# Local transformers: the feed-forward's normalisation moved onto tokens, with new orders of work

## The chip, the cores and the metric

One core of a Trainium2 chip runs the whole kernel. The metric is the device time of one execution in microseconds (us); the median of three is given. The profile is one further execution, taken by the hardware profiler.

## What is computed

Eight layers act on x of 8 sequences x 256 tokens x 128 channels; before each, x is normalised over its channels, and the layer's result is added to x. Layers 2 and 4 are the same local transformer of six blocks (`DEPTH`). One block is, for each sequence (`LN_EPS` is 1e-5):

```
x = attn_layer(shift_tokens(x), Wqkv, q_scale, k_scale, Wo) + x
t = shift_tokens(x)                      # the upper 64 channels come from the token before
mu  = t.mean(-1);  var = ((t - mu)**2).mean(-1)
xn  = (t - mu) / sqrt(var + 1e-5) * g + bln
a, gate = split(xn @ W1 + b1)
x = (a * gelu(gate)) @ W2 + b2 + x
```

The attention has 16 heads of 64 in windows of 32 tokens, l2-normalised and rotated queries and keys, and a softmax. The other layers are a state-space scan, a dense and a linear attention, a per-head attention and two quantised feed-forward layers. The change touches the local transformers, and the normalisation that stands ahead of every one of the eight layers.

## The kernel before

**Layout.** In the local transformer activations lie with channels on the partitions and tokens along the free dimension (`net.zT`, 128 x 256 for a sequence). There are 48 sequence-blocks (`SEQS` = 6 blocks x 8 sequences) in each of the two layers, and each passes through the stages below. `pipeline` (L1031) runs 54 iterations on every engine. In iteration n a step with lag k works on sequence-block n - k, so `run(score, 4, 0)` is the score product of block n - 4. Five engines each have an `iteration` with an order written out by hand; they are coupled by semaphores alone, and an engine works strictly in its order. Lag 2 to 4 is shift, projection, rotation and turning of q and k; lag 4 and 5 scores, softmax and the weighted sum; lag 6 the output projection and the feed-forward.

**TensorE (L1356 and on).** Twelve projections of 512 columns (`project`, `project_v`), four `turn_qk` and four `turn_probs` (16 transposes of 64 rows each), four `score`, four `weigh`, two halves of `out_project`, three `up`, one `down`. The 512-column products run as two matmuls on two halves of the output partitions (`COLUMNS`). The lists `PROJECTIONS` and `PAIRS_OF_BANKS` state in which order the PSUM banks are handed on, and so what each product waits for.

**The feed-forward's normalisation.** `out_project` leaves the attention's output in the PSUM bank `fb`. On VectorE `residual1` (L1571) makes three additions: the shifted residual `xs2` in two halves of 64 channels, and the unshifted residual `z1`. On TensorE `centre` (L1307) multiplies `xs2` by the centring matrix. On ScalarE `square2` (L1440) writes the square and a copy `cen`. `variance` (L1314) sums the squares with four narrow products, `add_eps` (VectorE), `std` and `spread_std` (POOL: a power, and a diagonal matrix 128 x 256) follow, and `spread` (L1322) multiplies ones by that diagonal, which puts each token's factor on all partitions. `affine` (VectorE, L1585) multiplies it by gain and `cen`; `bias_xn` (ScalarE) adds the bias and writes `xn`, the input of `up`.

**The layers' normalisation.** `normalise` (L243) treats 2048 tokens as four quarters. Last in it TensorE spreads the factors for quarters 0 and 1, then 2 and 3, and VectorE multiplies quarter after quarter (L348 to L351).

**SyncE.** `next_wo`, `next_w1`, `next_w2`, `next_wqkv` (L1072 to L1098) reload weights once per block of eight sequences, each behind the last use of the old ones, and `move_v` moves parts of v.

## Time and profile before

| | us |
|---|---|
| median of 3 executions | 4160.24 (4156.2 to 4161.15) |
| the profiled execution, its own time | 4153.05 |
| its span in the profile | 4151.3 |
| TensorE busy | 3819.6 (92%) |
| VectorE / ScalarE / POOL busy | 3628.6 / 3311.8 / 3092.3 |

The two local transformers take the stretches from about 492 to 2057 us and from about 2204 to 3770 us. PE is TensorE's matmul, PEld its weight load, DVE VectorE, ACT ScalarE, POOL GpSimd and SP SyncE. A view of the timeline gives the start, the duration, the engine, the line, the output and inputs, the count, and in brackets the idle time ahead of it with what ended it. Durations of successive instructions on one engine overlap, so the cost of one is read as the distance to the next one's start. An fp32 matmul shows as two records, a transpose as one.

### The profile page before, as it was taken

What the parts mean: (1) busy time and instruction counts of PE and PEld (TensorE: products, weight loads), DVE (VectorE), ACT (ScalarE), POOL (GpSimd) and SP (SyncE); (2) the same over time, 40 slices, a digit from 0 to 9 for tenths busy, and PEclk for the clock granted to TensorE, in tenths of its full rate; (3) what the DMA queues carried; (4) which work ended last, traced back from release to release, by engine and by line L of the source; (5) the groups of instructions that cost most, each with busy time, mean ns of one, the idle gap of its engine ahead of it and who ended that gap; (6) DMA issues with size and microseconds to landing.
All of it is one profiled execution on the core that took longest, in us unless ns stands there. A gap on an engine that the chain in (4) does not pass through costs nothing. (4 is left out here: it accounts for less than half of the span.)

```text
span 4151.3 us, 141232 instructions
## 1 busy us (share of the span) xinstructions
PE 3819.6 (92%) x52643; PEld 2278.6 (55%) x52643; DVE 3628.6 (87%) x11433; ACT 3311.8 (80%) x10465; POOL 3092.3 (74%) x3901
## 2 busy tenths in 40 slices
PE   5888889999999999999867999999999999996686
PEld 2333356666666666666553666666666666663464
DVE  7999899999999999999477999999999999984646
ACT  6888589999999999999515999999999999983122
POOL 3999788888888888888396888888888888862324
PEclk8999999999999999999998999999999999997888
DMA  1000111111111111111002111111111111110000
GB/s 29 1 1 1 48 25 26 50 33 28 53 28 43 41 36 38 30 41 26 20 0 58 31 28 43 38 43 33 38 43 28 50 33 31 30 33 3 6 3 11
DMA packets 78607, 122.74 MB, mean 30 GB/s; under 512 B 26024, under 2 KB 47204, under 8 KB 77924
## 3 DMA queue, kind: packets, MB, share of 16 engines
q1 hardware_dynamic: 77924, 113.71, 10.2%
q8 instruction: 419, 6.86, 0.7%
q14 instruction: 264, 2.16, 0.2%
HBM read 35.56 MB, written 1.05 MB: 9 GB/s over the span
## 5 line engine op out<-in xcount | busy, mean ns | idle before, releaser
L1123 POOL TENSOR_TENSOR local_qk<-local_qk,local_rb 128x512 f32<-128x512 f32 x768 | 977.4, 1278 | 228.5 <-DVE local_rb L1532 228.0
L1420 ACT ACTIVATE local_pr<-local_tb,local_nmax 128x96 f32<-128x96 f32 x3072 | 1002.2, 355 | 126.7 <-DVE local_nmax L1551 116.1
L1551 DVE CUSTOM_DVE_ANT_0 local_tb<-local_tb,local_mask,local_rinv 128x96 f32<-128x96 f32 x3072 | 785.4, 319 | 78.6 <-PE local_tb L1253 75.5
L1228 PE MATMUL local_pj<-local_wqkv,local_xs 128*64 128x512 f32 x3072 | 797.6, 609 | 29.0 <-DVE local_xs L1516 15.0
L1157 POOL TENSOR_TENSOR local_pr<-local_pr,local_rsum 128x384 f32<-128x384 f32 x768 | 622.8, 827 | 194.9 <-DVE local_rsum L1558 194.9
L1420 ACT ACTIVATION_READ_ACCUMULATOR local_pr<-local_tb,local_nmax 128x1 f32 x3072 | 676.5, 221 | 0.0
L1529 DVE TENSOR_TENSOR local_qk<-local_pj,local_rope 128x512 f32<-128x512 f32 x768 | 524.0, 682 | 97.7 <-ACT local_sq L1403 94.4
L1403 ACT ACTIVATE local_sq<-local_pj 128x512 f32<-128x512 f32 x768 | 472.6, 615 | 111.5 <-PE local_pj L1228 111.5
L1532 DVE TENSOR_TENSOR local_rb<-local_pj,local_rope 128x512 f32<-128x512 f32 x768 | 523.3, 681 | 0.7 <-POOL local_qk L1123 0.7
L1539 DVE TENSOR_REDUCE local_ss<-local_sq 128x8 f32<-128x512 f32 x768 | 519.3, 677 | 0.0
L1277 PEld LDWEIGHTS local_ob<-local_prT,local_v 128*64 128x64 f32 x12288 | 414.9, 138 | 175.5 <-issue 163.0
L1277 PE MATMUL local_ob<-local_prT,local_v 128*64 128x64 f32 x12288 | 428.2, 223 | 4.2 <-DVE local_oT L1568 4.2
L1551 DVE DVE_READ_ACCUMULATOR2_ANT local_nmax<- 128x1 f32 x3072 | 430.1, 140 | 2.0
L1428 ACT ACTIVATE local_prT<-local_tb 128x512 f32<-128x512 f32 x768 | 412.9, 634 | 0.7 <-PE local_tb L1264 0.5
L1239 PE MATMUL local_pj<-local_wqkv,local_xs 128*64 128x512 f32 x1536 | 400.8, 600 | 1.6 <-DVE local_rb L1532 1.6
L1129 POOL TENSOR_TENSOR local_qk<-local_qk,local_rinv 128x512 f32<-128x512 f32 x384 | 396.3, 1042 | 0.0
L1253 PEld LDWEIGHTS local_tb<-local_kT,local_qT 64*64 64x64 f32 x12288 | 266.2, 133 | 194.7 <-ACT local_prT L1428 76.3
L1302 PE MATMUL local_fb<-local_oT,local_wo 128*64 128x256 f32 x3072 | 368.0, 382 | 1.4 <-DVE net_zT L1601 1.4
L777 POOL TENSOR_TENSOR mamba_scan_drive<-mamba_u,mamba_scan_b_all 128x512 f32<-128x512 f32 x256 | 320.1, 1276 | 52.4 <-ACT mamba_scan_b_all L747 48.9
L1344 PE MATMUL local_fb<-local_xn,local_w 128*64 128x256 f32 x2304 | 313.1, 393 | 11.0 <-DVE local_g L1595 4.7
L1292 PEld LDWEIGHTS local_tb<-net_ident,local_qk 64*128 64x128 f32 x6144 | 221.3, 139 | 185.7 <-issue 147.9
L1253 PE MATMUL local_tb<-local_kT,local_qT 64*64 64x96 f32 x12288 | 320.6, 248 | 0.3 <-ACT local_kT L1437 0.3
(450 smaller groups left out, 7283.0 us busy)
## 6 DMA issues: line engine op xcount, KB each, us to landing
local_v<-local_v SPq DMA_DIRECT2D x288, 256.0 KB, 3.9
local_wqkv<-L_ffn_Wqkv_dram SPq DMA_DIRECT2D x72, 256.0 KB, 3.1
local_wo<-L_ffn_Wo_dram SPq DMA_DIRECT2D x12, 512.0 KB, 4.1
local_w<-L_ffn_W_dram SPq DMA_DIRECT2D x12, 341.0 KB, 3.0
mamba_parts<-mamba_in_low SPq DMA_DIRECT2D x24, 64.0 KB, 2.0
local_w<-L_ffn_W_dram SPq DMA_DIRECT2D x12, 128.0 KB
y_dram<-store_xtok SPq DMA_DIRECT2D x4, 256.0 KB, 2.8
local_oT<-rope_dram SPq DMA_DIRECT2D x2, 256.0 KB, 2.7
```

The source lines that it names most:

```text
L1123: nc.gpsimd.tensor_tensor(qk[:, u, :], qk[:, u, :], rb[:, u % 2, :], ALU.add).then_inc(s["summed"], 1)
L1157: nc.gpsimd.tensor_tensor(at, at, view(rsum[:, k // 2, k % 2, 0:1], [[1, 4], [0, KW]]), ALU.mult).then_inc(s["weighted"], 1)
L1228: ins = nc.tensor.matmul(bank[own, :], xs[:, par, u // 4 * P + own.start:u // 4 * P + own.stop], wqkv[:, dep % 2, u % 4 * BANK:(u % 4 + 1) ...
L1253: ins = nc.tensor.matmul(sc[h][low * QB:(low + 1) * QB, i * KW:(i + 1) * KW], qT[own, par, p, q:q + QB], kT[own, par, p, q:q + KW], start= ...
L1277: ins = nc.tensor.matmul(ob[h * DH:(h + 1) * DH, i * P + low * QB:i * P + (low + 1) * QB], v[:, par, V_BLOCK[2 * t + low], 2 * (4 * half + ...
L1403: nc.scalar.activation(sq[:, u % 2, :], projection_bank("rotated", u)[:, :], ACT.Square).then_inc(s["squared"], 1)
L1420: ins = nc.scalar.activation(pr[:, (NU * c + k) % PR_RING, i, WIN:WIN + KW], scores[:, i * KW:(i + 1) * KW], ACT.Exp, scale=-1.0, bias=nma ...
L1428: nc.scalar.activation(prT[:, kk % PT_RING, low, :], pair_of_banks("probs", kk)[low][:, :], ACT.Copy).then_inc(s["probs_copied"], 1)
L1529: nc.vector.tensor_tensor(heads8(qk[:, u, :]), heads8(bank[:, :]), cosines, ALU.mult)
L1532: nc.vector.tensor_tensor(rb[:, u % 2, :].rearrange("p (h a c) -> p h a c", a=2, c=DH // 2), swapped, sines, ALU.mult).then_inc(s["rotated ...
L1539: nc.vector.tensor_reduce(ss[:, par, 8 * u:8 * u + 8], heads8(sq[:, u % 2, :]), AX.X, ALU.add).then_inc(s["summed_sq"], 1)
L1551: ins = nc.vector.tensor_tensor_reduce(at, at, mask[:, k // 4, :], rinv[:, par, head:head + 1], 3.0e38, ALU.add, ALU.min, nmax[:, k, i:i + 1])
```

## The change

In the feed-forward the normalisation is done with tokens on the partitions. `residual1` makes one addition, into a `z1` with a column of zeros in front. `turn_z` transposes `z1` on TensorE in two halves of 64 channels; the upper half reads one column earlier, which is the shift. VectorE takes mean and variance of each of the two token tiles with `bn_stats` and `bn_aggr`. POOL adds epsilon, takes the power and makes scale and bias for each token (`affine`). ScalarE applies them (`scale_tokens`), `turn_x` transposes back, and `bias_xn` applies gain and bias for each channel. Since the bias comes out as plus mean times factor and the scale as minus the factor, POOL turns the sign of the gains once. `centre`, `variance`, `spread`, `square2`, `add_eps`, `spread_std` and the old `affine` are gone. All five hand-written orders and the two bank lists are new. In `normalise` the pairs are (0,3) and (1,2), and quarter 3 is multiplied on POOL from a copy that ScalarE makes.

```diff
+SPREAD_PAIRS = ((0, 3), (1, 2))
@@ normalise
+            pool.wait_ge(moved, 1)
+            pool.wait_ge(kept, NC)
+            nc.gpsimd.tensor_tensor(part(z, NC - 1), part(z, NC - 1), part(sq, NC - 1), ALU.mult)
...
-            for pair in ((0, 1), (2, 3)):
+            for pair in SPREAD_PAIRS:
...
+            act.wait_ge(spread, 1)
+            nc.scalar.activation(part(sq, NC - 1), p_bc[:, NC - 1, :], ACT.Copy).then_inc(moved, 1)
...
-            for q in range(NC):
+            for q in range(NC - 1):
                 dve.wait_ge(kept, q + 1)
-                dve.wait_ge(spread, q // 2 + 1)
+                dve.wait_ge(spread, 1 if q == 0 else 2)
@@ lists
+PAIRS_OF_BANKS = [("qk", 4, 1), ("probs", 5, 1), ("score", 4, 0), ("probs", 5, 2), ("qk", 4, 2), ("qk", 4, 3),
+         ("probs", 5, 3), ("qk", 3, 0), ("probs", 4, 0), ("score", 4, 1), ("score", 4, 2), ("score", 4, 3)]
+PROJECTIONS = [("rotated", 3, 2), ("v_ready", 4, 2), ("v_ready", 4, 3), ("rotated", 3, 3), ("rotated", 3, 4), ("rotated", 3, 5),
+         ("rotated", 3, 6), ("rotated", 3, 7), ("rotated", 2, 0), ("v_ready", 3, 0), ("v_ready", 3, 1), ("rotated", 2, 1)]
@@ SyncE iteration
                 run(move_v, 0, 0)
+                run(next_w1, 2, 0)
+                run(next_w2, 2, 0)
                 run(next_wo, 1, 0)
-                run(next_w1, 1, 0)
                 run(next_wqkv, -1, 0)
-                run(next_w2, 1, 0)
@@ POOL
             def std(e, par, _):
+                pool.wait_ge(s["var_in"], 2 * e + 2)
+                need(pool, s["tokens_ready"], e)
+                nc.gpsimd.tensor_scalar(deviation[:, :], mean_var[:, :, 1], LN_EPS, None, ALU.add).then_inc(s["eps_added"], 1)
+                pool.wait_ge(s["eps_added"], e + 1)
+                nc.gpsimd.tensor_tensor(rstd[:, :], deviation[:, :], net.minus_half[:, 0:2], ALU.pow).then_inc(s["root_ready"], 1)
+                pool.wait_ge(s["root_ready"], e + 1)
+                nc.gpsimd.tensor_tensor(affine[:, :, :], view(mean_var[:, 0, 0:1], [[3, 2], [2, 2]]), view(rstd[:, 0:1], [[1, 2], [0, 2]]),
+                                        ALU.mult).then_inc(s["std_ready"], 1)
@@ TensorE
+            def turn_z(e, par, h):
+                rows = COLUMNS[h]
+                if h:
+                    pe.wait_ge(s["z1_turned"], 2 * e + 1)
+                else:
+                    pe.wait_ge(s["z1_ready"], e + 1)
                 for t in range(2):
+                    ins = nc.tensor.transpose(fb[:, t * P + rows.start:t * P + rows.stop], z1[rows, par, 1 - h + t * P:1 - h + (t + 1) * P], net.ident[rows, rows])
+                ins.then_inc(s["z1_turned"], 1)
+
+            def turn_x(e, par, h):
...
+                    ins = nc.tensor.transpose(fb[:, L + t * P + rows.start:L + t * P + rows.stop], xt[rows, t, :], net.ident[rows, rows])
@@ TensorE iteration, whole, in its new order
+ out_project 6,1 | project 3,2 | turn_z 6,0 | turn_qk 4,1 | turn_z 6,1 | turn_probs 5,1 | project_v 4,2
+ score 4,0 | weigh 5,0 | project_v 4,3 | project 3,3 | weigh 5,1 | project 3,4 | turn_probs 5,2
+ turn_x 6,0 | turn_qk 4,2 | turn_x 6,1 | project 3,5 | weigh 5,2 | up 6,0 | project 3,6 | turn_qk 4,3
+ turn_probs 5,3 | up 6,1 | project 3,7 | turn_qk 3,0 | turn_probs 4,0 | project 2,0 | up 6,2
+ score 4,1 | score 4,2 | project_v 3,0 | down 6,0 | weigh 5,3 | project_v 3,1 | score 4,3
+ project 2,1 | out_project 5,0
@@ ScalarE
+            def scale_tokens(e, par, _):
+                act.wait_ge(s["std_ready"], e + 1)
+                need(act, s["x_turned"], 2 * e)
+                for t in range(2):
+                    ins = nc.scalar.activation(xt[:, t, :], fb[:, t * P:(t + 1) * P], ACT.Identity, scale=affine[:, t, 1:2], bias=affine[:, t, 0:1])
+                ins.then_inc(s["tokens_ready"], 1)
@@ VectorE
+                need(dve, s["z1_turned"], 2 * (e - 1))
                 need(dve, s["z_ready"], B + e - 1)
+                nc.vector.tensor_tensor(z1[:, e % 2, 1:1 + L], z[:, e % B, :], fb[:, 0:L], ALU.add).then_inc(s["z1_ready"], 1)
+
+            def stats(e, par, _):
+                dve.wait_ge(s["z1_turned"], 2 * e + 2)
+                for t in range(2):
+                    nc.vector.bn_stats(moments[:, t, :], fb[:, t * P:(t + 1) * P]).then_inc(s["moments_ready"], 1)
+
+            def aggregate(e, par, _):
+                for t in range(2):
+                    dve.wait_ge(s["moments_ready"], 2 * e + t + 1)
+                    need(dve, s["std_ready"], e)
+                    nc.vector.bn_aggr(mean_var[:, t, 0:2], moments[:, t, :]).then_inc(s["var_in"], 1)
@@ VectorE iteration, whole, in its new order (ss is sum_squares)
+ maxima 5,7 | recip 5,2 | rotate 3,1 | residual1 6,0 | ss 3,1 | recip 5,3 | ss 3,2 | stats | aggregate
+ rotate 3,2 | maxima 4,0 | copy_o 5,0 | maxima 4,1 | shift_in 2,0 | rotate 3,3 | ss 3,3 | copy_o 5,1
+ recip 4,0 | rotate 3,4 | ss 3,4 | copy_o 5,2 | rotate 3,5 | ss 3,5 | rotate 3,6 | ss 3,6 | gate 6,0
+ ss 3,7 | rotate 3,7 | gate 6,1 | gate 6,2 | maxima 4,2 | maxima 4,3 | rotate 2,0 | maxima 4,4
+ maxima 4,5 | residual2 6,0 | copy_o 5,3 | maxima 4,6 | ss 2,0 | recip 4,1
```

ScalarE's new order begins with the copies of the last turns and the squares, then `exps` 5,2 to 5,7, and has `scale_tokens` ahead of `exps` 4,0 and `bias_xn` ahead of `square` 3,5. The table of exp and that of gelu are still each loaded once in an iteration.

## Rows read from the trace of the kernel before

**Rows 1.** The page, part 1: busy time, share of the span, instructions.
```profile
PE 3819.6 (92%) x52643; PEld 2278.6 (55%) x52643; DVE 3628.6 (87%) x11433; ACT 3311.8 (80%) x10465; POOL 3092.3 (74%) x3901
```
**Rows 2.** Windows: busy time of each engine in one period of 31.42 us.
```profile
core 0: us, PE busy (x) PEld busy (x) DVE busy (x) ACT busy (x) POOL busy (x), PEclk, DMA share, GB/s
985.00:1016.42 31.42, 31.42 (x520) 19.39 (x518) 29.46 (x107) 29.40 (x102) 25.53 (x36) 1.00 0.13 36
```
**Rows 3.** Line L1450 (`bias_xn`) in two stretches of the second transformer: first and last start.
```profile
L1450 ACT ACTIVATE local_xn<-local_fb,local_cols x4: 474/474/476, 2299.3 to 2393.6; 128x256 f32<-128x256 f32 x4
...
L1450 ACT ACTIVATE local_xn<-local_fb,local_cols x2: 473/473/473, 3735.0 to 3755.8; 128x256 f32<-128x256 f32 x2
```
**Rows 4.** Timeline of PE: the three products that go, and their neighbours.
```profile
1020.07 0.60 PE L1311 MATMUL local_fb<-local_xs,net_center 128*64 128x256 f32 x4
1020.60 0.89 PE L1253 MATMUL local_tb<-local_kT,local_qT 64*64 64x96 f32 x32
...
1022.40 0.35 PE L1318 MATMUL local_fb<-net_mean,local_sq 128*64 128x1 f32 x8
1022.61 1.92 PE L1228 MATMUL local_pj<-local_wqkv,local_xs 128*64 128x512 f32 x8
...
1025.28 0.60 PE L1326 MATMUL local_fb<-local_diag,net_ones 128*64 128x256 f32 x4
1025.82 0.71 PE L1292 MATMUL local_tb<-net_ident,local_qk 64*128 64x64 f32 x16
1026.37 0.67 PE L1264 MATMUL local_tb<-net_ident,local_pr 64*128 64x64 f32 x16
```
**Rows 5.** The page, part 5: the costliest weight loads of a turn.
```profile
L1292 PEld LDWEIGHTS local_tb<-net_ident,local_qk 64*128 64x128 f32 x6144 | 221.3, 139 | 185.7 <-issue 147.9
```
**Rows 6.** Timeline of DVE: what goes (additions, affine) in one period.
```profile
1018.25 0.86 DVE L1576 TENSOR_TENSOR local_xs<-net_zT,local_fb 64x256 f32<-64x256 f32 x2
1019.14 0.42 DVE L1578 TENSOR_TENSOR local_z<-net_zT,local_fb 128x256 f32<-128x256 f32 x1
...
1025.94 0.49 DVE L1589 SCALAR_TENSOR_TENSOR local_fb<-local_fb,local_cols,local_cen 128x256 f32<-128x256 f32 x1
```
**Rows 7.** Timeline of ACT: `square2`, and what follows its copy (left out).
```profile
1020.71 0.40 ACT L1442 ACTIVATE local_sq<-local_fb 128x256 f32<-128x256 f32 x1
...
1021.26 0.62 ACT L1411 ACTIVATE local_v<-local_pj 128x512 f32<-128x512 f32 x1
```
**Rows 8.** Timeline of POOL: the diagonal matrix.
```profile
1023.83 0.61 POOL L1151 TENSOR_TENSOR local_diag<-net_ident,local_deviation 128x256 f32<-128x256 f32 x1
```
**Rows 9.** Timeline of PE, around the end of the feed-forward.
```profile
1003.86 1.55 PE L1253 MATMUL local_tb<-local_kT,local_qT 64*64 64x96 f32 x64
1005.34 1.08 PE L1344 MATMUL local_fb<-local_xn,local_w 128*64 128x256 f32 x8
1006.25 1.03 PE L1239 MATMUL local_pj<-local_wqkv,local_xs 128*64 128x512 f32 x4
...
1012.05 0.71 PE L1292 MATMUL local_tb<-net_ident,local_qk 64*128 64x64 f32 x16
```
**Rows 10.** Timeline of DVE in the same stretch: gates, one unit of maxima, `residual2`.
```profile
1006.74 0.86 DVE L1595 SCALAR_TENSOR_TENSOR local_g<-local_fb,local_cols,local_g 128x256 f32<-128x256 f32 x2
1007.53 0.31 DVE L1551 CUSTOM_DVE_ANT_0 local_tb<-local_tb,local_mask,local_rinv 128x96 f32<-128x96 f32 x1
...
1008.47 0.85 DVE L1516 TENSOR_REDUCE local_xs<-net_zT 64x256 f32<-64x256 f32 x2
...
1010.42 0.48 DVE L1601 SCALAR_TENSOR_TENSOR net_zT<-local_fb,local_cols,local_z 128x256 f32<-128x256 f32 x1
```
**Rows 11.** The end of `normalise` ahead of the second transformer: timelines of ACT and DVE.
```profile
2200.48 1.08 ACT L328 ACTIVATE net_zT<-local_ln_p_cen 128x512 f32<-128x512 f32 x2
...
2201.92 2.48 DVE L351 TENSOR_TENSOR net_zT<-net_zT,local_ln_p_bc 128x512 f32<-128x512 f32 x4 [2.03 <-PE local_ln_p_bc L319]
```
**Rows 12.** The page, part 5: a POOL product of 128x512.
```profile
L1123 POOL TENSOR_TENSOR local_qk<-local_qk,local_rb 128x512 f32<-128x512 f32 x768 | 977.4, 1278 | 228.5 <-DVE local_rb L1532 228.0
```

More of the change, by code:

```diff
@@ L264, in normalise @@
         p_weights = p_bc[:, 1, :]
[L265 to L266 removed]
+        cleared, centred, squared, summed, kept, roots, turned, copied, spread, moved = (
+            net.sem(f"{tag}_ln_{n}") for n in ("cleared", "centred", "squared", "summed", "kept", "roots", "turned", "copied", "spread", "moved"))
         x = net.xT[:, :, :].rearrange("p b l -> p (b l)")
@@ L1175, in iteration @@
                 run(scale, 4, 2)
-                run(scale, 4, 3)
                 run(norm_p, 5, 2)
                 run(norm_p, 5, 3)
+                run(scale, 4, 3)
                 run(add_parts, 3, 0)
@@ L1181, in iteration @@
                 run(norm_p, 5, 4)
+                run(std, 6, 0)
+                run(norm_p, 5, 5)
                 run(add_parts, 3, 1)
+                run(add_parts, 3, 2)
+                run(norm_p, 5, 6)
                 run(scale, 4, 7)
-                run(norm_p, 5, 5)
-                run(add_parts, 3, 2)
-                run(std, 6, 0)
-                run(spread_std, 6, 0)
                 run(add_parts, 3, 3)
-                run(norm_p, 5, 6)
-                run(add_parts, 3, 4)
                 run(norm_p, 5, 7)
@@ L1193, in iteration @@
                 run(norm_p, 4, 1)
+                run(add_parts, 3, 4)
                 run(add_parts, 3, 5)
@@ L1477, in iteration @@
                 run(copy_probs, 5, 2)
+                run(copy_v, 4, 2)
                 run(copy_probs, 5, 3)
-                run(square2, 6, 0)
-                run(copy_v, 4, 1)
+                run(scale_tokens, 6, 0)
                 run(exps, 4, 0)
+                run(copy_v, 4, 3)
                 run(square, 3, 3)
@@ L1484, in iteration @@
                 run(square, 3, 4)
-                run(bias_xn, 6, 0)
-                run(copy_qk, 4, 4)
-                run(copy_qk, 4, 5)
                 run(copy_probs, 5, 4)
                 run(copy_probs, 5, 5)
+                run(copy_qk, 4, 4)
+                run(bias_xn, 6, 0)
                 run(square, 3, 5)
+                run(copy_qk, 4, 5)
                 run(gelu, 6, 0)
+                run(gelu, 6, 1)
                 run(square, 3, 6)
@@ L1607, in iteration @@
             def iteration(run):
-                run(add_eps, 6, 0)
+                run(maxima, 5, 7)
+                run(recip, 5, 2)
+                run(rotate, 3, 1)
+                run(residual1, 6, 0)
+                run(sum_squares, 3, 1)
+                run(recip, 5, 3)
+                run(sum_squares, 3, 2)
+                run(stats, 6, 0)
+                run(aggregate, 6, 0)
+                run(rotate, 3, 2)
+                run(maxima, 4, 0)
                 run(copy_o, 5, 0)
-                run(recip, 5, 3)
                 run(maxima, 4, 1)
+                run(shift_in, 2, 0)
                 run(rotate, 3, 3)
-                run(affine, 6, 0)
                 run(sum_squares, 3, 3)
+                run(copy_o, 5, 1)
+                run(recip, 4, 0)
                 run(rotate, 3, 4)
-                run(recip, 4, 0)
-                run(copy_o, 5, 1)
                 run(sum_squares, 3, 4)
+                run(copy_o, 5, 2)
                 run(rotate, 3, 5)
```

175 lines of the change are left out of this document (63 added, 112 removed).

## The prediction

> **What bounds the kernel now.** I read the page's first part, then windows over one period of the local transformer, then the timeline of each engine in that period. The page makes TensorE the busiest engine, with VectorE near it [rows 1]. A share over the span mixes stages, so the next view is one period of the pipeline: in 31.42 us TensorE has no idle time at all, at a granted clock of 1.00; VectorE is busy 29.46 us, ScalarE 29.40, POOL 25.53 [rows 2]. Busy TensorE might still hide waits, since the ends of matmuls are modelled, so I looked at distances between starts: a 16-transpose group costs 0.55 us wherever another such group follows, and the whole sequence repeats without a gap. So one period is TensorE's own work, and what is taken from TensorE comes off the time, as long as VectorE (1.96 us of slack) and ScalarE (2.02 us) can follow.
>
> How many periods count: the first `bias_xn` of the second transformer starts at 2299.3 and the 47th at 3735.0 [rows 3]. That is 1435.7 us for 46 distances, which is 45 at 31.42 and one short one of 22 in the drain. With two transformers 90 periods are bound by TensorE. Filling and draining are not, for there the engines wait for each other in turn.
>
> **What TensorE loses.** `centre` holds it from 1020.07 to 1020.60, 0.53 us; `variance` from 1022.40 to 1022.61, 0.21; `spread` from 1025.28 to 1025.82, 0.54 [rows 4]. Together 1.28 us in a period.
>
> **What TensorE gains.** Four groups of two transposes (`turn_z` twice, `turn_x` twice), eight in all, each with 64 rows and 128 columns of weights and 64 moving columns: the very form of `turn_qk`. There 16 take 0.55 us [rows 4], 0.034 us each. But `turn_qk` alternates between the lower and the upper 64 rows, so that two run side by side; each half has 8 in 0.55 us, 0.069 us each. The new groups keep to one half. The lower bound is 0.034 each, 0.28 us in all, if they slip beside the turns of the other half, next to which the new order puts them. The upper bound takes the whole duration of such a weight load, 0.139 us [rows 5], for each of the eight: 1.11 us. I take 0.069, the rate that one half is seen to keep: 0.55 us. TensorE's period becomes 31.42 - 1.28 + 0.55 = 30.69, a gain of 0.73 us.
>
> Against this stands a rule. The trace shows eight weight loads of 0.139 us for one half inside 0.55 us [rows 4, 5], so they overlap with something of their own half or end early. The Trainium skill (TensorE: Matmul & The Clock Gate, Part 3, The mechanism) says that a weight load overlaps running matmuls only where its row group differs, and its section on LDWEIGHTS makes 128 columns about 107 ns. By that the eight would cost at least 0.86 us and the gain would be 0.42 us a period. The trace of `turn_qk` does not bear it out, since one half would then need 0.86 us where 0.55 is measured; the result it points to is weighed as the first rival.
>
> **VectorE.** Gone are the two half additions, 1018.25 to 1019.14, 0.89 us, and the affine, about 0.40 of its 0.49 [rows 6], and the narrow `add_eps`, left out of the sum; the third addition of 0.42 stays. New are two `bn_stats` over 128 elements and two `bn_aggr` over 6. The trace has neither. Nearest are a 256-element addition at 0.42 [rows 6] as an upper end, and a unit of four maxima over 96 elements each, 0.94 us or 0.24 apiece [rows 10], as the lower end for the first. I take 0.25 for a `bn_stats` and 0.18 for a `bn_aggr`: 0.86 in all, 1.7 at worst. VectorE loses 1.3 and gains 0.86: from 29.46 to about 29.0, at worst 29.9. Still under 30.69.
>
> **ScalarE.** `square2` with its copy holds it from 1020.71 to 1021.26, 0.55 us [rows 7]. `scale_tokens` is two activations of 128 elements with two per-partition operands; a 256-element one costs 0.27 to 0.40 [rows 7], so two cost 0.4 to 0.8, taken as 0.55. Even. `bias_xn` gets a scale operand, at most 0.1. The two table loads stay two. So ScalarE remains at about 29.4 of 30.69: its slack shrinks from 2.0 to 1.3 us. This is the thinnest place of the forecast.
>
> **POOL.** The 0.61 us diagonal [rows 8] goes, two operations on 2 and 4 elements with a wait between come, about 0.5. With 25.5 us of 31.42 it has room. Nothing gained or lost; queued behind `std` are `norm_p` 5,5 and additions, due several us later. The sign of the gains is turned once, while filling.
>
> **The new waits on TensorE.** An engine in a fixed order stands still if one operand is late, so I walked three places of the new order. First, `out_project` 5,0 now closes the iteration and needs `residual2`. From the end of `up` 6,2 TensorE has two scores, 1.48, and then the same six groups as between 1006.25 and 1012.05, 5.80: 7.28 us [rows 9]. VectorE meanwhile does two gates, 0.79, four units of maxima at 0.94, one rotation of two 512-element operations at 0.62 [rows 11], and `residual2`, 0.48 [rows 10]: 6.27, and 0.1 for the signal. Margin 0.9 us; before, VectorE had only two units of maxima and `shift_in` there. Second, `turn_z` 6,0 stands one projection behind (0.9, as the `up` from 1005.34 to 1006.25 [rows 9], both four fp32 records' worth of 512 columns) `out_project`: signal, addition 0.42, signal, about 0.6. Margin 0.3, if VectorE is free by then. Third, the chain from `turn_z` through statistics, POOL and `scale_tokens` has nine groups of TensorE, 0.55 to 0.93 us each, some 7 us, before `turn_x`, and needs about 3.5 plus POOL's queue. None of them stops TensorE by my count, but none is wide. Each costs its overrun 90 times.
>
> **SyncE.** The reloads of w1 and w2 are issued ahead of that of wo and one step later in SyncE's order, and `move_v` of the next block stands behind them. All of them are waited for in the order in which TensorE uses the weights up, once in eight periods, and have most of a period before the next use; the DMA engines are busy for 0.13 of the time [rows 2]. Cost nothing; if the cover fails, a few us ten times in the run.
>
> **`normalise`, eight times.** VectorE multiplies four quarters from 2201.92 for 2.48 us, to 2204.40 [rows 11]. With three it ends at about 2203.8. ScalarE is free at 2201.56 [rows 11], copies the fourth in 0.6 from 2201.92, and POOL's product of 128x512, 1.28 us [rows 12], ends at about 2203.9. So 0.5 us eight times, 4 us; from nothing (POOL slow to start) to 5.
>
> **The sum.** 90 x 0.73 = 66, plus 4, is 70 us. Filling and draining are taken as even, with 5 us to either side: the chain of the last block loses two products and gains two turns with waits. The profiled execution has 4153.05 us around a span of 4151.3; it would become about 4083. The median before, 4160.24, lies 7 above it, and the same saving gives 4090.
>
> **Rivals.** A measurement of this kernel can tell about 0.2%, 8 us, from no change.
>
> *Turns are dear.* Each of the eight waits for its own weight load, 0.139 us [rows 5]. TensorE's period is 31.42 - 1.28 + 1.11 = 31.25: 90 x 0.17 = 15, with 4 of `normalise` 19 us, 4141. For it speaks that two in a row share a half, against it the 0.55 us of `turn_qk`. Chance 0.12. The skill's rule above, at 107 ns, would land between this and the forecast.
>
> *ScalarE becomes the bound.* It idles 2.02 us a period now [rows 2], while TensorE never does. If the waits of the new order leave it as much, its period is 29.4 + 2.0 = 31.4, nothing is gained in the pipeline, and only the 4 us of `normalise` remain: 4156. TensorE would then show idle time of 0.7 us a period. For it: the slack is short and exps and maxima wait for each other. Against: most of that idle time is waiting for TensorE's products, which come sooner. Chance 0.08; the change would in effect not do what it says.
>
> *`out_project` waits for `residual2`.* The margin of 0.9 us above is used up by VectorE running late behind gates and maxima, which wait for `gelu` and so for ScalarE. It has to be late by 0.9 + 0.73 = 1.6 us to cost more than is gained; at 2.0 the period is 31.8, so 90 x 0.4 = 36 slower, less 4: 4192. Chance 0.08.
>
> **How the numbers follow.** The forecast, 4090, has a chance of 0.72. Its own range runs from 4060 (turns at 0.034: 90 x 1.0 = 90, `normalise` 5, ends 5) to about 4120 (half of the gain lost to small waits). The range of 8 in 10 reaches on to the dear turns: 4060 to 4141. Faster by over 0.2%: forecast, dear turns and a little of the second rival, 0.86. Within 0.2%: the rest of the second, 0.06. Slower: 0.08.
>
> **What will show it.** Windows of one period after: a period near 30.7 with TensorE still without idle time. The timeline of TensorE: each pair of turns 0.14 us to the next start; 0.28 would be the dear case. VectorE near 29.0, ScalarE near 29.4 busy. The waits: no long one of `out_project` for `residual2`, nor of `turn_z` for `z1`. The last quarter of `normalise` ending 0.5 us earlier. I am wrong if TensorE idles by over 0.3 us a period, or if `bn_stats` takes over 0.5 us.

## The result and the profile after

The changed kernel takes 4095.95 us (median of 4 executions, 4093.34 to 4099.39) against 4158.22 for the kernel before on the same chip (4155.48 to 4161.15): a ratio of 0.9852, 95% interval 0.984 to 0.9864. The forecast was 4090, the range 4060 to 4141. The profiled execution has 4093.68 us around a span of 4091.9.

The page's first part, against [rows 1]:

```profile
PE 3767.2 (92%) x51875; PEld 2247.0 (55%) x51875; DVE 3550.8 (87%) x11427; ACT 3327.1 (81%) x10473; POOL 3075.6 (75%) x4007
```

The view of windows, one period of the first local transformer (busy time by engine, then TensorE's granted clock, the DMA share and GB/s), against [rows 2]:

```profile
973.38:1004.13 30.75, 30.75 (x511) 19.02 (x508) 28.72 (x108) 29.47 (x103) 25.23 (x36) 1.00 0.14 37
```

TensorE still shows no idle time, and the period is 30.75 us where it was 31.42; 30.69 was forecast. I took the period as the distance from one `down` to the next. It is flat for 40 distances of the first transformer, then come three of 31.2, then the drain. From the first product of its normalisation to that of the next layer each transformer takes less by 28.8 and 29.9 us, 58.7 together. The other layers together take 0.7 us less, the rest of the 59.4 by which the spans differ.

The new operations, from a view that groups instructions (count | busy us, mean ns of one | idle time before), stretch 599 to 1890 us:

```profile
L1451 ACT ACTIVATE local_xt<-local_fb,local_affine 128x128 f32<-128x128 f32 x84 | 33.9, 455 | 24.4 <-POOL local_affine L1158 24.4
...
L1459 ACT ACTIVATE local_xn<-local_fb,local_cols 128x256 f32<-128x256 f32 x42 | 28.5, 678 | 0.0
...
L1589 DVE BATCH_NORM_STATS2 local_moments<-local_fb 128x6 f32<-128x128 f32 x84 | 20.4, 284 | 0.0
```

The last row of the three gives `bn_stats` 0.284 us; the first says that ScalarE stood idle for 24.4 us in 42 periods, 0.58 each, ahead of `scale_tokens`, until POOL's last step of `std`.

The turns on TensorE, timeline of one period, `turn_z` (L1323) between and beside `turn_qk` (L1301):

```profile
977.80 0.27 PE L1323 MATMUL local_fb<-net_ident,local_z 64*128 64x64 f32 x1
977.81 0.27 PE L1301 MATMUL local_tb<-net_ident,local_qk 64*128 64x64 f32 x1
977.91 0.22 PE L1323 MATMUL local_fb<-net_ident,local_z 64*128 64x64 f32 x1
977.92 0.65 PE L1301 MATMUL local_tb<-net_ident,local_qk 64*128 64x64 f32 x14
...
978.47 0.67 PE L1273 MATMUL local_tb<-net_ident,local_pr 64*128 64x64 f32 x16
```

Twenty turns take from 977.80 to 978.47, 0.67 us, where the sixteen of `turn_qk` take 0.55: four `turn_z` cost 0.12. And `turn_x` (L1333), on both sides of `turn_qk` 4,2:

```profile
986.04 0.28 PE L1333 MATMUL local_fb<-net_ident,local_xt 64*128 64x64 f32 x2
986.26 0.71 PE L1301 MATMUL local_tb<-net_ident,local_qk 64*128 64x64 f32 x16
986.82 0.28 PE L1333 MATMUL local_fb<-net_ident,local_xt 64*128 64x64 f32 x2
987.03 0.65 PE L1237 MATMUL local_pj<-local_wqkv,local_xs 128*64 128x512 f32 x2
```

From 986.04 to 986.26 and from 986.82 to 987.03, 0.22 and 0.21. The eight turns take 0.12 + 0.22 + 0.21 = 0.55 us of the starts, as forecast. How much of that is turns the experiments had to say.

The end of a block, the first walked wait: VectorE's `residual2` (L1607), and TensorE's `out_project` (L1311).

```profile
1002.73 0.48 DVE L1607 SCALAR_TENSOR_TENSOR net_zT<-local_fb,local_cols,local_z 128x256 f32<-128x256 f32 x1
...
1004.13 1.25 PE L1311 MATMUL local_fb<-local_oT,local_wo 128*64 128x256 f32 x10
```

From the end of `residual2` (1003.21) to the start of `out_project` 0.9 us lie, the forecast's margin to the tenth.

### The profile page after: what moved, and what is told of

Read it like the earlier page. It is cut to its first block and busy times, and to the rows that moved or that the text cites. A ratio compares the mean times of both kernels' runs of the same rounds, so it can differ in the third digit from the quotient of the medians.

```text
span 4091.9 us, 139809 instructions
## 1 busy us (share of the span) xinstructions
PE 3767.2 (92%) x51875; PEld 2247.0 (55%) x51875; DVE 3550.8 (87%) x11427; ACT 3327.1 (81%) x10473; POOL 3075.6 (75%) x4007
## 5 line engine op out<-in xcount | busy, mean ns | idle before, releaser
L1237 PE MATMUL local_pj<-local_wqkv,local_xs 128*64 128x512 f32 x3072 | 814.1, 609 | 21.5 <-DVE local_rb L1541 8.3
L1164 POOL TENSOR_TENSOR local_pr<-local_pr,local_rsum 128x384 f32<-128x384 f32 x768 | 623.0, 828 | 274.4 <-DVE local_rsum L1567 274.4
L1560 DVE CUSTOM_DVE_ANT_0 local_tb<-local_tb,local_mask,local_rinv 128x96 f32<-128x96 f32 x3072 | 772.6, 319 | 14.5 <-PE local_tb L1262 14.0
L1427 ACT ACTIVATION_READ_ACCUMULATOR local_pr<-local_tb,local_nmax 128x1 f32 x3072 | 753.1, 245 | 0.0
L1410 ACT ACTIVATE local_sq<-local_pj 128x512 f32<-128x512 f32 x768 | 491.6, 640 | 55.6 <-PE local_pj L1237 55.3
L1435 ACT ACTIVATE local_prT<-local_tb 128x512 f32<-128x512 f32 x768 | 457.2, 639 | 5.7 <-PE local_tb L1273 5.7
L1248 PE MATMUL local_pj<-local_wqkv,local_xs 128*64 128x512 f32 x1536 | 410.5, 613 | 4.4 <-DVE local_rb L1541 4.2
L1311 PE MATMUL local_fb<-local_oT,local_wo 128*64 128x256 f32 x3072 | 348.0, 379 | 0.0
L1262 PE MATMUL local_tb<-local_kT,local_qT 64*64 64x96 f32 x12288 | 329.2, 250 | 3.3 <-ACT local_pr L1427 1.8
L1301 PEld LDWEIGHTS local_tb<-net_ident,local_qk 64*128 64x128 f32 x6144 | 231.5, 139 | 183.1 <-issue 82.3
```

Source lines behind the costliest of these rows:

```text
L1164: nc.gpsimd.tensor_tensor(at, at, view(rsum[:, k // 2, k % 2, 0:1], [[1, 4], [0, KW]]), ALU.mult).then_inc(s["weighted"], 1)
L1237: ins = nc.tensor.matmul(bank[own, :], xs[:, par, u // 4 * P + own.start:u // 4 * P + own.stop], wqkv[:, dep % 2, u % 4 * BANK:(u % 4 + 1) ...
L1262: ins = nc.tensor.matmul(sc[h][low * QB:(low + 1) * QB, i * KW:(i + 1) * KW], qT[own, par, p, q:q + QB], kT[own, par, p, q:q + KW], start= ...
L1410: nc.scalar.activation(sq[:, u % 2, :], projection_bank("rotated", u)[:, :], ACT.Square).then_inc(s["squared"], 1)
L1427: ins = nc.scalar.activation(pr[:, (NU * c + k) % PR_RING, i, WIN:WIN + KW], scores[:, i * KW:(i + 1) * KW], ACT.Exp, scale=-1.0, bias=nma ...
L1435: nc.scalar.activation(prT[:, kk % PT_RING, low, :], pair_of_banks("probs", kk)[low][:, :], ACT.Copy).then_inc(s["probs_copied"], 1)
```

## The experiments

Each period below is the distance between starts of `down` in the flat part of the first transformer. By the forecast's count 90 such periods bind; the starts of before show 44 full ones in each transformer, 88 in all. Costs below are distances between starts, group by group.

| kernel | period, us | median, us |
|---|---|---|
| before | 31.42 | 4158.6 |
| after | 30.75 | 4095.95 |
| norm_old | 30.75 | 4101.84 |
| old_orders | 32.0 | 4197.37 |
| turns_twice | 30.85 | 4101.34 |
| x_round_probs | 30.76 | 4092.15 |
| std_first | 30.39 | 4063.61 |
| std_first_x_round | 30.52 | 4069.24 |
| std_first_x_round_late | 30.52 | 4069.3 |
| tensor_more | 31.59 | 4174.75 |
| std_first_turns_twice | 30.85 | 4103.5 |
| std_first_scalar_more1 | 30.85 | 4107.04 |
| std_first_scalar_more4 | 32.22 | 4231.59 |
| before_std_first | 31.42 | 4159.54 |

**norm_old.** The end of `normalise` as before, all else as after.

```diff
-SPREAD_PAIRS = ((0, 3), (1, 2))
+SPREAD_PAIRS = ((0, 1), (2, 3))
@@ normalise: no copy on ScalarE, no product on POOL
-            for q in range(NC - 1):
+            for q in range(NC):
                 dve.wait_ge(kept, q + 1)
-                dve.wait_ge(spread, 1 if q == 0 else 2)
+                dve.wait_ge(spread, q // 2 + 1)
```

> The changed kernel (median 4096) with the end of normalise as before: pairs (0,1) and (2,3), VectorE multiplies all four quarters, no copy by ScalarE, no product on POOL. My theory: the new end is worth 0.58 us in each of eight places (TensorE's idle time behind the spreading products falls from 2.34 to 1.76 us in the traces), so this run idles 2.34 again and is 4.6 us slower than the changed kernel, about 4100.5; the period of the transformers stays 30.74 us. Rival: the next stage waits for something else than the last quarter, and the time stays at 4096.

Measured: 4101.84 us, ratio to before 0.9864 (0.9849 to 0.9878). The median is 5.9 above that of the changed kernel, less than the intervals can part, so the trace has to tell. TensorE's first projection behind the normalisation, timeline of after and then of norm_old:

```profile
2175.67 3.68 PE L1237 MATMUL local_pj<-local_wqkv,local_xs 128*64 128x512 f32 x8 [2.76 <-DVE local_xs L1525]
```

```profile
2179.94 3.46 PE L1232 MATMUL local_pj<-local_wqkv,local_xs 128*64 128x512 f32 x8 [3.34 <-DVE local_xs L1520]
```

The wait is 3.34 - 2.76 = 0.58 us shorter with three quarters on VectorE and the fourth on POOL: eight times 0.58 is 4.6 us. This part works by itself, as forecast (0.5 each).

**old_orders.** The new steps, with TensorE, ScalarE, VectorE and POOL each in its order of before (SyncE and `normalise` keep the new one): `turn_z` where `centre` stood, `turn_x` about `turn_qk` 4,2 where `spread` stood, `scale_tokens` ahead of `exps` 4,1, and so on. An extract:

```diff
@@ TensorE
                 run(project_v, 4, 1)
-                run(centre, 6, 0)
+                run(turn_z, 6, 0)
...
-                run(variance, 6, 0)
...
-                run(spread, 6, 0)
+                run(turn_x, 6, 0)
                 run(turn_qk, 4, 2)
+                run(turn_x, 6, 1)
```

> The new steps of the feed-forward set into the five hand-written orders and the two bank lists of before (turn_z ahead of and behind score 4,0, turn_x about turn_qk 4,2, statistics where add_eps stood, scale_tokens ahead of exps 4,1, bias_xn one copy later). My theory: TensorE's work is the bound and is 30.7 to 30.8 us a period here too, but the chain from turn_z through statistics, POOL and ScalarE to turn_x has only about 5 us between score 4,0 and up 6,0 where it needs over 3.5 and queues, so TensorE waits 0.3 to 0.7 us a period: period 31.0 to 31.5, 4125 to 4165. Rival A: the gain comes from the products that are gone alone, and the period is 30.75, 4096. Rival B: the new steps without new orders lose more than they gain, period over 31.6, above 4175.

Measured: 4197.37 us, ratio 1.0096 (1.0081 to 1.0111), a period of 32.0. That is slower than before: the steps take work from TensorE and yet lengthen the period by 0.6 us. ScalarE's timeline shows one cause, TensorE's under it where the time goes:

```profile
1030.11 0.63 ACT L1418 ACTIVATE local_v<-local_pj 128x512 f32<-128x512 f32 x1
1031.93 0.34 ACT L1427 ACTIVATE local_pr<-local_tb,local_nmax 128x96 f32<-128x96 f32 x1 [1.20 <-DVE local_nmax L1560]
```

```profile
1029.57 0.34 PE L1323 MATMUL local_fb<-net_ident,local_z 64*128 64x64 f32 x2
1029.84 0.89 PE L1262 MATMUL local_tb<-local_kT,local_qT 64*64 64x96 f32 x32
...
1035.42 0.29 PE L1333 MATMUL local_fb<-net_ident,local_xt 64*128 64x64 f32 x2
1036.05 0.71 PE L1273 MATMUL local_tb<-net_ident,local_pr 64*128 64x64 f32 x16 [0.34 <-ACT local_pr L1427]
```

ScalarE waits 1.2 us for the maxima, and TensorE then for the exps. This alone doesn't explain the loss: the waits for maxima sum to 43.4 us in 1000, against 35.4 in the kernel before, some 0.3 us a period more. TensorE's starts against those of before account for the 0.6. The products that go give back 1.27. `turn_z` takes 0.53, its two pairs at 0.27 each, where it stands alone between products (0.12 in all beside `turn_qk` in the changed kernel); `turn_x` with `turn_qk` 4,2 takes 1.29 for the 0.55 of `turn_qk` alone, with the wait for the exps in it; `weigh` 5,1 takes 1.13 for 0.93 to the start of `turn_x`, which waits there for `scale_tokens`; `turn_probs` 5,3 and 4,0 take 1.32 for 1.13; the others together 0.2 more. So the change is two things: the steps, which lose 0.6 us a period in the old orders, and the orders, which bring 1.25 once the steps are there. The old steps in the new orders were not run. My expectation had the wait of `turn_x` and put it too small, and it missed the rest; the rival was right.

**turns_twice.** Each `turn_z` and `turn_x` issued twice, sixteen turns for eight.

```diff
-                for t in range(2):
+                for t in (0, 1, 0, 1):
                     ins = nc.tensor.transpose(fb[:, t * P + rows.start...
```

> Each of the eight turns of the feed-forward is issued twice, so a period has 16. My reading of the trace after: turns beside those of the other half cost 0.03 us each (turn_z), those alone 0.06 (turn_x); so eight more cost 4 x 0.03 + 4 x 0.06, about 0.36 us, up to 0.55 at 0.069 each: period 31.1 to 31.3, 4129 to 4146. Rival (a weight load of 0.139 us not overlapped): 1.11 us more, period 31.85, 4196. Second rival (the period is set by ScalarE, not by TensorE): no more than 0.1, 4105.

Measured: 4101.34 us, 0.9867 (0.9851 to 0.9883), period 30.85. Eight more turns cost 0.10 us, not 0.36 to 0.55. So some of the changed kernel's 0.55 us is not turns but standing still behind them, time into which more turns fit, as the second rival had it. By the starts the four more of `turn_z` cost 0.24; `turn_x` with `turn_qk` 4,2 takes 0.96 with eight turns where it takes 0.99 with four; and 0.10 of waits further on are gone (`score` 4,1 and 4,2 1.48 for 1.55, `turn_probs` 4,0 0.59 for 0.62). The rows of `turn_x` above agree: from 986.04 to 986.26 for two turns that TensorE takes elsewhere at 0.06 apiece, and what follows is `turn_qk` 4,2, whose PSUM bank has held scores until `exps` 4,1 has read them.

**x_round_probs.** `turn_x` 0 and 1 each one step earlier.

```diff
+                run(turn_x, 6, 0)
                 run(turn_probs, 5, 2)
-                run(turn_x, 6, 0)
-                run(turn_qk, 4, 2)
                 run(turn_x, 6, 1)
+                run(turn_qk, 4, 2)
```

> In TensorE's order turn_x 0, turn_probs 5,2, turn_x 1, turn_qk 4,2 in place of turn_probs 5,2, turn_x 0, turn_qk 4,2, turn_x 1. In the trace after, turn_qk 4,2 starts its weight loads 0.21 us behind the last one of turn_x 0, just when exps 4,1 ends on ScalarE; everywhere else the next load follows in 0.06 to 0.12. My theory: that is a wait of 0.1 to 0.15 us for the bank of the scores, hidden by the modelled ends of the matmuls; with both turn_x ahead of turn_qk it falls away and turn_x overlaps as turn_z does: period 30.6, 12 us faster than the changed kernel, 4084. Rival: the gap is a cost of changing between the two kinds of turn, and the period stays at 30.74, 4096.

Measured: 4092.15 us, 0.9842 (0.9827 to 0.9856), period 30.76. The period is the same and the medians lie within their intervals: `turn_qk` 4,2 starts when it did (986.24 here), only the wait has moved, and the 0.12 us gained behind it are lost again, 0.09 of them ahead of `up` 6,1. TensorE's order doesn't set this moment; ScalarE does.

**What holds ScalarE.** POOL's timeline in the changed kernel, and under it ScalarE's:

```profile
974.79 1.61 POOL L1164 TENSOR_TENSOR local_pr<-local_pr,local_rsum 128x384 f32<-128x384 f32 x2 [2.63 <-DVE local_rsum L1567]
...
979.59 0.83 POOL L1164 TENSOR_TENSOR local_pr<-local_pr,local_rsum 128x384 f32<-128x384 f32 x1
980.50 0.22 POOL L1154 TENSOR_SCALAR local_deviation<-local_mean_var 128x2 f32<-128x2 f32 x1
980.81 0.72 POOL L1156 TENSOR_TENSOR local_rstd<-local_deviation,net_minus_half 128x2 f32<-128x2 f32 x1
981.61 0.20 POOL L1158 TENSOR_TENSOR local_affine<-local_mean_var,local_rstd 128x4 f32<-128x4 f32 x1
...
981.84 0.81 ACT L1451 ACTIVATE local_xt<-local_fb,local_affine 128x128 f32<-128x128 f32 x2 [0.56 <-POOL local_affine L1158]
```

VectorE's `bn_aggr` is done at 979.85. POOL, which is idle 2.63 us five steps earlier and works without a pause from there, is then in `norm_p` 5,4 (979.59, L1164), and takes up `std` only at 980.50. ScalarE waits 0.56 us for it, and has no idle time from there to past `exps` 4,1, for which `turn_qk` 4,2 waits.

**std_first.** One line moved: POOL's `std` ahead of `norm_p` 5,4.

```diff
                 run(scale, 4, 6)
-                run(norm_p, 5, 4)
                 run(std, 6, 0)
+                run(norm_p, 5, 4)
                 run(norm_p, 5, 5)
```

> POOL's std of the next block runs ahead of norm_p 5,4 instead of behind it: it no longer waits out the 2.7 us that norm_p waits for VectorE's reciprocal, so ScalarE's scale_tokens starts 0.4 to 0.6 us earlier. Theory A (the period of 30.75 us is closed by a ring POOL - ScalarE - TensorE - VectorE in which this step lies): the period falls to 30.60 to 30.68 us and the kernel to about 4080 to 4090 us. Theory B (TensorE's own work closes it, 30.4 us of products with some 0.3 us of waits that have other ends): period 30.75, kernel 4096 us within 2. Price of the move: norm_p 5,4 comes some 0.6 us later, and if the value products wait for it, the period grows by as much (31.0 or more, 4120 us).

Measured: 4063.61 us (4060.9 to 4066.67), 0.977 (0.9755 to 0.9785), a period of 30.39: 0.36 less than after, and 90 x 0.36 = 32 is the difference of the medians. (From the first `down` to the last the two transformers take 32.6 us less.) POOL, ScalarE and TensorE in one period of it, three timelines:

```profile
976.84 0.22 POOL L1154 TENSOR_SCALAR local_deviation<-local_mean_var 128x2 f32<-128x2 f32 x1 [0.26 <-DVE local_mean_var L1595]
...
978.17 0.81 ACT L1451 ACTIVATE local_xt<-local_fb,local_affine 128x128 f32<-128x128 f32 x2
...
982.93 0.22 PE L1333 MATMUL local_fb<-net_ident,local_xt 64*128 64x64 f32 x1
982.93 0.22 PE L1301 MATMUL local_tb<-net_ident,local_qk 64*128 64x64 f32 x1
982.99 0.22 PE L1333 MATMUL local_fb<-net_ident,local_xt 64*128 64x64 f32 x1
983.00 0.66 PE L1301 MATMUL local_tb<-net_ident,local_qk 64*128 64x64 f32 x14
...
983.65 1.08 PE L1237 MATMUL local_pj<-local_wqkv,local_xs 128*64 128x512 f32 x4
```

Now POOL waits for the variance (0.26), not the variance for POOL; ScalarE waits for nothing ahead of `scale_tokens`; and `turn_x` and `turn_qk` run side by side as `turn_z` does: 982.93 to 983.65, 0.72 us, where the changed kernel needs from 986.04 to 987.03, 0.99. That is 0.27 of the 0.36. The rest is in two later groups of TensorE, `score` 4,1 and 4,2 with 1.50 for 1.55 and `turn_probs` 4,0 with 0.59 for 0.62. Theory A held in its mechanism and was too small in size, since it counted only the wait of 0.13 us, not that the turns would interleave.

**before_std_first.** The same move in the kernel before.

```diff
+                run(std, 6, 0)
+                run(spread_std, 6, 0)
                 run(norm_p, 5, 5)
                 run(add_parts, 3, 2)
-                run(std, 6, 0)
-                run(spread_std, 6, 0)
```

> The kernel before with its own std and spread_std moved ahead of norm_p 5,5. There POOL reaches std before the variance is there (it waits 0.2 us), so if the 0.36 us a period that std_first gave came from a wait that the change's own order made, this move gives nothing: 4158 us within 3. If an earlier std is worth as much in any order of this kernel, 4126 us.

Measured: 4159.54 us, 1.0001 (0.9991 to 1.0011). The wait that std_first takes away is one that the change's own POOL order had made.

**std_first_x_round.** std_first with the order of x_round_probs.

> The same move, and TensorE's turn_x 0 and 1 stand one step earlier, ahead of turn_probs 5,2 and turn_qk 4,2. Theory A: with ScalarE earlier, the wait of 0.13 us behind turn_x 0 is gone as well: period 30.50 to 30.62, kernel 4074 to 4084 us. Theory B: nothing, 4092 us as with the order alone.

Measured: 4069.24 us, 0.9782 (0.9768 to 0.9797), period 30.52: inside theory A's range for the period and below it for the median, but against std_first, which was not known when it was written, the step costs 0.13. `turn_qk` 4,2, whose copy ScalarE makes next, starts 0.12 us later in the period, and TensorE loses 0.05 at `turn_probs` 4,0 (0.64 to the next start, 0.59 in std_first) and 0.06 at `score` (1.56 for 1.50). That the first brings about the second is my reading; no run takes them apart.

**std_first_x_round_late.** In the last eight sequence-blocks of a transformer `residual2` adds its result into net.xT as well. That addition moves to the end of VectorE's iteration.

```diff
-                if f >= SEQS - B: ... net.xT += z        # in residual2
+            def into_x(f, par, _): ...                    # the same addition
...
+                run(into_x, 6, 0)                         # last in the iteration
```

> As std_first_x_round, with VectorE's addition into net.xT (there for the last eight blocks of each transformer only) moved from behind residual2 to the end of VectorE's iteration. If that addition of 0.47 us is what lengthened three of the last periods to 31.2 us, those three are again as long as the others and the kernel is 2 to 3 us below std_first_x_round; if the stretch has another cause, no difference.

Measured: 4069.3 us, 0.9783 (0.9767 to 0.9799). The three distances that were 30.72 to 30.74 are 30.52 to 30.53 as all others; so the addition is what stretched them (by 0.46 us in the changed kernel). There the loss isn't at `out_project`, which takes its usual 3.45. It begins where `turn_qk` 4,1 lags behind `turn_z` and no longer runs beside it, timeline of after:

```profile
1838.65 0.33 PE L1323 MATMUL local_fb<-net_ident,local_z 64*128 64x64 f32 x2
1838.87 0.71 PE L1301 MATMUL local_tb<-net_ident,local_qk 64*128 64x64 f32 x16
```

From `turn_z` to `project_v` 4,2 it is 1.48 for 1.27, and `weigh` 5,1 takes 1.14 for 0.93. By which of VectorE's later steps the addition comes through to these two was not tried. The kernel is no faster: the last distance of the drain is 22.6 us in the first transformer where it was 20.9, and 20.9 as before in the second, which is 1.1 us shorter. That distance also comes out differently in the two transformers of other kernels (20.6 and 22.5 in norm_old), so it doesn't speak against the move. My expectation of 2 to 3 us less was a miss.

**tensor_more.** Part 0 of `up` issued twice.

```diff
-                for i, (half, j) in enumerate((...)[part]):
+                for i, (half, j) in (2 if part == 0 else 1) * list(enumerate((...)[part])):
```

> Part 0 of the up products is issued twice in each iteration: TensorE has some 0.87 us more work in a period. If TensorE's own work closes the period, it grows by 0.8 to 0.9 us, to 31.6; if a ring through ScalarE closes it with 0.3 us of hidden room on TensorE, by 0.5 to 0.6, to 31.3; if TensorE has a microsecond of room, not at all. Over 90 periods: 4145 to 4178 us.

Measured: 4174.75 us (one execution), period 31.59, 0.84 longer for 0.87 of work. TensorE has no room at this place.

**std_first_turns_twice.** Sixteen turns, on top of std_first.

> std_first (period 30.39 us) with all eight turns of a block issued twice. In std_first the four turn_z cost TensorE 0.12 us and the four turn_x 0.19 us of the distance between their neighbours' starts, 0.31 together, where after.py had 0.55 with waits for ScalarE in it. If a turn's own price is those 0.04 us, the period grows by 0.30 to 0.35 us, to 30.7; if it is the 0.069 us of the forecast, by 0.55, to 30.94; if waits still cover them, by 0.1 as in turns_twice.

Measured: 4103.5 us (one execution), period 30.85, 0.46 longer: 0.058 us a turn. The first `turn_x` in its timeline, now in fours:

```profile
990.55 0.28 PE L1333 MATMUL local_fb<-net_ident,local_xt 64*128 64x64 f32 x2
990.62 0.27 PE L1301 MATMUL local_tb<-net_ident,local_qk 64*128 64x64 f32 x1
990.67 0.23 PE L1333 MATMUL local_fb<-net_ident,local_xt 64*128 64x64 f32 x1
990.73 0.22 PE L1301 MATMUL local_tb<-net_ident,local_qk 64*128 64x64 f32 x1
```

Starts follow each other at 0.05 to 0.06 us. The eight turns of std_first itself cost 0.12 + (0.72 - 0.55 = 0.17) = 0.29, 0.036 each, beside turns of the other half; further ones cost 0.058. The outcome lies between the two values expected. The period is that of turns_twice, where `std` stands in its later place, and group by group the starts are the same to 0.01 us: with the turns doubled `turn_qk` 4,2 waits for nothing, and moving `std` is worth nothing.

**std_first_scalar_more1 and 4.** One or four more activations of 256 elements ahead of `bias_xn`, into a spare tile, on top of std_first.

```diff
+                for i in range(1):      # 4 in the other kernel
+                    nc.scalar.activation(spare[:, i, :], fb[:, L:2 * L], ACT.Identity, scale=cols[...], bias=cols[...])
                 nc.scalar.activation(xn[:, :], fb[:, L:2 * L], ACT.Identity, ...)
```

> std_first with one more ScalarE activation of 256 elements (0.44 us) in front of bias_xn. ScalarE is busy 29.47 us of 30.39. Theory A (TensorE's work now closes the period, ScalarE has some 0.9 us of room): period grows by no more than 0.1 us. Theory B (ScalarE is already the ring's tightest part): it grows by 0.4 us, to 30.8.

> The same with four of them: 1.76 us more on ScalarE. With 0.9 us of room the period becomes 31.2 to 31.3 us (the kernel 4140 us); with no room 32.1 us (4220 us); with 2 us of room 30.4 us.

Measured: periods of 30.85 and 32.22, 0.46 and 1.83 longer (one execution each). By the starts an added activation is 0.45 us, so the work is 0.45 and 1.80. Theory A fell: the 0.8 us that ScalarE idles in a period are no room. ScalarE and TensorE of the first, timelines:

```profile
988.86 0.58 ACT L1461 ACTIVATE local_spare<-local_fb,local_cols 128x256 f32<-128x256 f32 x1
989.31 0.59 ACT L1462 ACTIVATE local_xn<-local_fb,local_cols 128x256 f32<-128x256 f32 x1
...
988.83 1.10 PE L1287 MATMUL local_ob<-local_prT,local_v 128*64 128x64 f32 x32
989.95 1.08 PE L1351 MATMUL local_fb<-local_xn,local_w 128*64 128x256 f32 x8
```

`weigh` to `up` 6,0 takes 1.12 us for 0.93 in std_first: xn comes 0.19 late for an activation of 0.45, so its margin was about 0.25. The other 0.27 are small waits behind it (`up` 6,0 0.92 for 0.87, `turn_probs` 5,3 0.71 for 0.59, 4,0 0.64 for 0.59, `score` 1.56 for 1.50). With four the first interval is 2.48, that is 1.55 more, 1.80 less 0.25, and the others stay at 0.28.

## Why the prediction was right, and where it was not

**What bounds the kernel.** TensorE without a pause on the page, a period as long as its work: that carried the forecast. But the sentence that a period "is TensorE's own work", with what the other engines have left over as slack, was too simple. tensor_more lengthens the period by nearly all that it adds to TensorE, std_first_turns_twice by 0.058 us for each further turn, scalar_more1 by all that it adds to ScalarE, and moving one POOL step shortens it by 0.36 us. The period is one path that passes through both engines several times; TensorE's waits at those passages are of 0.03 to 0.13 us, which the view of the waits doesn't list for it, and the busy time of 30.75 in 30.75 covers them. Only starts compared group by group between two kernels show them.

**The count of periods.** The forecast read [rows 3] as 45 distances of 31.42 and one of 22. The trace has 44, then 29.1 and 24.3, so 88 full periods and not 90. The gain of two periods is 1.3 us, less than the spread between runs.

**TensorE's loss** of 1.28 us went as counted. **TensorE's gain**: 0.55 forecast, 0.55 in the starts, and the forecast was right by the sum, not by its reason: that part is luck. Its sign, each pair 0.14 us to the next start, came nowhere: the pairs of `turn_z` take 0.06, those of `turn_x` 0.22 and 0.21. The turns themselves cost 0.29 (as std_first shows), which is the forecast's lower bound of 0.28, taken "if they slip beside the turns of the other half". The other quarter of a microsecond was a wait for ScalarE of some 0.1 us, which also kept `turn_x` and `turn_qk` 4,2 from running side by side. Beside it, the projections in the new order stand more often ahead of transposes (11.17 for 10.89 us for the twelve), +0.28. `turn_qk` costs 0.18 less, since two of its four groups stood ahead of products at 0.64 and now all stand ahead of other turns at 0.55; the remaining groups cost 0.07 less. To two places: -1.27 + 0.56 + 0.28 - 0.18 - 0.07 = -0.68.

**The first rival and its rule.** The rival's 0.139 us a turn did not come in this kernel. It nearly did in old_orders, 0.13 a turn for `turn_z` (1029.57 to 1029.84 for two): what kept the turns cheap is that the new order sets them beside other turns. As to the rule that a load overlaps running matmuls only in another row group (the Trainium skill, TensorE: Matmul & The Clock Gate, Part 3, The mechanism): the trace of std_first_turns_twice has two turns of the same half ahead of all others (990.55 x2, which last 0.28 us together where one lasts 0.22), so 0.06 us apart, and a further turn costs 0.058 us. By the page's figure of 107 ns eight further turns would cost up to 0.86, an estimate; they cost 0.46. The trace does not agree, and decides. The same section also lets a load run ahead into a background weight buffer, whatever its row group; no run shows whether that is what happens here.

**VectorE** went from 29.46 to 28.72 busy, forecast 29.0: two `bn_stats` take 0.48 from first start to last end (0.50 forecast), two `bn_aggr` 0.30 (0.36 forecast); to the next start it is 0.40 and 0.22.

**ScalarE**, called the thinnest place: 29.47 busy, forecast 29.4. `bias_xn` and what follows it, timelines of before and of after:

```profile
1026.46 0.48 ACT L1450 ACTIVATE local_xn<-local_fb,local_cols 128x256 f32<-128x256 f32 x1
1026.84 1.07 ACT L1437 ACTIVATE local_qT<-local_tb 128x512 f32<-128x512 f32 x2
```

```profile
987.94 0.68 ACT L1459 ACTIVATE local_xn<-local_fb,local_cols 128x256 f32<-128x256 f32 x1
988.38 0.72 ACT L1410 ACTIVATE local_sq<-local_pj 128x512 f32<-128x512 f32 x1
```

The records last 0.68 and 0.48, but to the next start it is 0.45 (the median of 39) and 0.37: the scale operand costs 0.08, within the forecast's 0.1. `scale_tokens` takes 0.70 to the next start for two, where 0.55 was forecast. That the place was thin was right. What the forecast lacked is that the margin lies in single hand-overs, 0.25 us at xn (in std_first), not in the 1.3 us of idle time.

**POOL, the step that failed.** The forecast said "Nothing gained or lost" and gave the chain from `turn_z` to `turn_x` "some 7 us" against "about 3.5 plus POOL's queue". It looked for who waits behind `std` on POOL, and never for what `std` waits for there. It stands behind `norm_p` 5,4, and the work from there back to a wait of 2.63 us for VectorE's reciprocal has no pause. The chain itself had room (xt was ready at about 982.65, TensorE asked for it at 986.04), so `turn_x` didn't wait; but `exps` 4,0 and 4,1 stand behind `scale_tokens` on ScalarE, and `turn_qk` 4,2 waits for those. 32 us lay there.

**The other walked waits** held: `out_project` with its margin of 0.9, `turn_z` without a long wait. The rival on `residual2` needed 1.6 us of lateness and had none. VectorE running late did cost something in three of the last periods of each transformer, where a second addition of 0.4 us follows `residual2`: +0.46 each, not forecast, and not at `out_project`. It cost nothing in the end, since the drain became shorter by about as much (its last three distances sum to 69.3 us for 70.8): from the first `down` to the last the first transformer takes 30.05 us less, 45 x 0.67 = 30.2.

**The second rival** (ScalarE's waits take the gain away) is in kind what old_orders shows, with TensorE's turns at their dear price on top. That it didn't happen here is the orders' doing. The forecast priced the steps in the new orders only, and so did not say that the steps in the old ones lose 0.6 us a period.

**`normalise`**: 4 forecast, 4.6 by the trace. **The sum**: 90 x 0.67 = 60.3 and 4.6 are 64.9; the profiled spans differ by 4151.3 - 4091.9 = 59.4. Of the 5.5 us between, half are in the transformers: in the first, 30.05 of the distances and 0.58 of `normalise` make 30.6, and 28.8 came, the difference in filling and leaving the pipeline; in the second the distances themselves sum to 29.3 less. The other half is in the other layers, where six `normalise` would give 3.5 and 0.7 came. The linear attention there took 2.0 us longer; over the kernels of this record it takes 86.2 to 89.0 us. What makes these was not tried. And the centring products of the dense layer took 1.9 longer, of which its other stages gave 1.0 back. They ran at another clock (windows of after, then of before, at the same place of the layer):

```profile
2025.30:2030.30 5.00, 4.70 (x11) 1.58 (x8) 0.91 (x2) 0.60 (x1) 0.20 (x1) 0.50 0.18 52
```

```profile
2055.00:2060.00 5.00, 4.70 (x15) 1.71 (x13) 0.91 (x2) 1.19 (x2) 0.20 (x1) 0.86 0.11 30
```

A granted clock of 0.50 is the lower level, 1.2 GHz; before it was 0.86 on average over the window. This comes and goes with the kernels: in before and in std_first the starts of these products spread over 3.1 us, in after over 4.9. What decides it was not tried.

## What to carry to other kernels

An engine that shows no idle time can still wait: compare the distances between starts, group by group, with a place where the same group is known to run free, and lengthen it a little (twice the suspected step) to see if the time moves. Slack is the margin of one hand-over, not busy time against the period. For each step that moves, look in both directions in its engine's queue: who waits behind it, and what wait it stands behind itself. A tiny step on a lightly used engine (here 1.3 us of POOL's 25) belongs ahead of the long step that nobody needs yet, and orders written by hand must be made again whenever steps change.

## What the runs showed of the hardware

Transposes of 64 rows in one half start 0.06 us apart though each weight load lasts 0.139 us by the trace, and with the other half beside them the turns cost 0.036 us each (std_first). A pair alone between products of other kinds takes 0.27 us to the next start (old_orders); whether a wait is in that was not tried. An activation over 256 elements with both scale and bias from SBUF holds ScalarE for 0.45 us to the next start, in after and in std_first alike, and for 0.37 with the bias alone (before), though its record lasts 0.68, 0.58 and 0.48: the record isn't the cost. POOL takes 0.20 to 0.22 us for two to four elements, and 0.72 for raising two elements to a power.
